# Graph attention on one core: maximum and exponentials of a unit one unit earlier, weighted sums in another PSUM bank, two bank pairs for the first group sums, slot rows zeroed during the projections

## What is computed

```python
h = layer_norm(node_feature, ln1_g, ln1_b)
qkv = (h @ Wqkv + bqkv).reshape(N, 3, H, DH)          # N 625, H 8, DH 64
q = qkv[:, 0] * D ** (-0.5); k = qkv[:, 1]; v = qkv[:, 2]
logits = jnp.einsum('ehd,ehd->eh', q[src], k[dst])    # per edge
a = logits + dist_attn + path_attn
mx = jax.ops.segment_max(a, dst, num_segments=N)
e = jnp.exp(a - mx[dst])
s = jax.ops.segment_sum(e, dst, num_segments=N)
msg = v[src] * (e / s[dst])[:, :, None]
agg = jax.ops.segment_sum(msg, dst, num_segments=N).reshape(N, D)
x = agg @ Wo + bo
```

## Time and profile before

| | us |
|---|---|
| median of 3 runs | 859.73 (856.99 to 859.93) |
| the profiled execution, its own time | 858.02 |
| its span, first to last instruction | 856.4 |
| projections, up to the barrier | 0 to 94.6 |
| attention, up to the next barrier | 94.6 to 357.7 |
| PE, DVE, ACT, POOL busy | 703.6, 524.8, 421.7, 162.2 |

### The profile page before, as it was taken

How to read it: one execution, slowest core, us unless ns; L and a number is a source line. 1 busy time by engine, 2 the same in 40 slices (tenths; PEclk the granted TensorE clock), 3 DMA queues, 4 the chain that set the end, 5 groups by cost and what they waited for, 6 DMA issues and landing times. The chain is left out here.

```text
span 856.4 us, 14647 instructions
## 1 busy us (share of the span) xinstructions
PE 703.6 (82%) x4980; PEld 550.1 (64%) x4980; DVE 524.8 (61%) x1107; ACT 421.7 (49%) x689; POOL 162.2 (19%) x242
## 2 busy tenths in 40 slices
PE   3997506676666767599999999999999999999993
PEld 2663203354444444348988867987889899988782
DVE  6658415587677733264432265527888788888864
ACT  5235202466666644256444364215676666766740
POOL 7342425455445310000000000310000000000022
PEclk9999765599999965699999999999999999999998
DMA  8232774555666454250000204395677666777224
GB/s 273 64 58 33 181 117 132 174 158 160 174 158 172 155 187 158 59 200 1 1 1 1 74 3 146 122 340 192 216 240 234 219 216 237 256 234 236 88 58 142
DMA packets 104125, 125.63 MB, mean 147 GB/s; under 512 B 32370, under 2 KB 70028, under 8 KB 103532
## 3 DMA queue, kind: packets, MB, share of 16 engines
q1 hardware_dynamic: 96955, 115.06, 42.8%
q0 software_dynamic: 5600, 6.54, 3.4%
q10 hardware_dynamic: 1488, 3.01, 1.5%
HBM read 94.91 MB, written 29.67 MB: 145 GB/s over the span
## 5 line engine op out<-in xcount | busy, mean ns | idle before, releaser
L2128 PE MATMUL ps<-xT,w_hi 128*128 128x480 f32 (+7 forms) x512 | 110.1, 337 | 2.4 <-DVE hT L1947 2.2
L1021 PE MATMUL ps<-onehot,group_weights 128*32 128x314 bf16 x1272 | 63.1, 341 | 43.8 <-ACT sums_out L976 23.9
L919 DVE TENSOR_SCALAR onehot<-iota_h,windows 128x628 bf16<-128x628 f16 x212 | 75.0, 417 | 32.1 <-DMA windows<-window_scratch 16.6
L2128 PEld LDWEIGHTS ps<-xT,w_hi 128*128 128x128 f32 x512 | 82.0, 189 | 9.9 <-DVE hT L1947 4.1
L1021 PEld LDWEIGHTS ps<-onehot,group_weights 128*32 128x32 bf16 x1272 | 36.8, 110 | 69.4 <-issue 42.2
L1933 DVE TENSOR_TENSOR w_lo<-weights_far,w_hi 128x1024 fp32r<-128x1024 f32 x64 | 78.0, 1220 | 2.5 <-ACT w_hi L2043 2.2
L2130 PE MATMUL ps<-xT,w_lo 128*128 128x240 f32 (+7 forms) x512 | 74.5, 268 | 0.0
L2130 PEld LDWEIGHTS ps<-xT,w_lo 128*128 128x128 f32 x512 | 73.5, 190 | 1.5
L976 ACT ACTIVATE sums_out<-ps 128x628 f32<-128x628 f32 x53 | 36.8, 695 | 70.8 <-PE ps L1021 50.4
L940 DVE CUSTOM_DVE_ANT_0 weights<-sums_in,exponents 126x628 f32<-126x628 f32 x40 | 34.4, 861 | 57.3 <-issue 30.8
L2043 ACT ACTIVATE w_hi<-weights_far 128x1024 fp32r<-128x1024 f32 x64 | 67.2, 1052 | 0.0
(11 more groups left out here) (308 smaller groups left out, 1551.7 us busy)
## 6 DMA issues: line engine op xcount, KB each, us to landing
weights_far<-in_L_ffn_w SPq DMA_DIRECT2D x64, 512.0 KB, 5.9
sums_scratch<-sums_out SPq DMA_DIRECT2D x53, 314.0 KB
weights_near<-in_L_ffn_w SPq DMA_DIRECT2D x32, 512.0 KB, 3.6
sums_in<-sums_scratch SPq DMA_DIRECT2D x40, 309.1 KB
weights_near<-in_L_gnn_W SPq DMA_DIRECT2D x4, 1024.0 KB, 5.5
weights_near<-in_L_ffn_sw SPq DMA_DIRECT2D x8, 512.0 KB, 5.2
weights_near<-in_L_gnn_Wqkv SPq DMA_DIRECT2D x3, 1024.0 KB, 7.6
weights_ff<-in_L_gnn_W SPq DMA_DIRECT2D x1, 3072.0 KB, 14.2
```

The costliest lines, as they stand in the source:

```text
L919: dve.tensor_scalar(onehot[w % 3][:, j, :], iota_h, windows[:, w % RING, j, 1:2], None, ALU.is_equal)\
L1021: last = pe.matmul(psW[r, a, :], R[w % 3][:, j, :, part], onehot[w % 3][:, j, a * SH:(a + 1) * SH], start=part == 0, stop=part == 2)
L2128: pe.matmul(both(bank, cap), w[u % 2][0][:, c, cut], xT(r)[:, c, :, :], start=c == 0, stop=False)
```

## The change

- The unit loop has another order. ACT does `norm(u)`, `exps(u+1)`, `keep(u)`, then the copies of the unit's blocks. DVE does `weights(u)`, for even u `collect(u//2 - 1)`, `guards(u+1)`, then the group weights of the next unit's blocks. PE does the sums of the first block, then logits for odd u or weighted sums for even u, then `turn(u)` (not `turn(u-1)`), then the sums of the second block.
- `psO` lies in bank 7, beside the end of `psP`. `turn` therefore waits for the collecting (`o_moved`), and `logits` no longer does; `weighted_sums` no longer waits for the next exponentials.
- The first 14 blocks of sums use two bank pairs in turn, 4 and 5, and 6 and 7. From block 14 on there is one pair as before. `turn(0)` waits for the 14 copies. `exps(0)` and `guards(0)` come behind block 1.
- In the projections the low parts of rounds 1 and 2 are made by DVE and not by POOL, and DVE, ACT and PE have small changes of order there (values of tile 2 earlier, exponentials of round 2 earlier, four filler matmuls in place of three). Only four blocks of windows are loaded there; blocks 4 and 5 follow in the attention.
- The slot rows are zeroed in three pieces that ACT issues between the copies of queries and keys.
- SP starts the attention with the two stores of edge parts. It waits for them only ahead of the first window that needs them (block 20), and the five parameter loads come behind all units.

```diff
+LOADED = 4
+ZERO_AT = {1: (0, 8), 5: (8, 16), 13: (16, SLOTS // DH)}
...
 @@ projections
-            for w in range(0, AHEAD, 2):
+            for w in range(0, LOADED, 2):
                 load_groups(nc, sp, mybir.EngineType.SP, w, tab, rec2_d, windows, g_in)
...
-            low_part(1)
-            low_part(2)
...
+            def low_part(r):
+                b0, nb = ROUNDS[r]
+                dve.wait_ge(mid_ready, r + 1)
+                dve.tensor_tensor(parts[:, b0:b0 + nb, :, 6:6 + 3 * H - 2:3], rec_all[:, b0:b0 + nb, :, 2:REC],
+                                  parts[:, b0:b0 + nb, :, 5:5 + 3 * H - 1:3], ALU.subtract).then_inc(lo_ready, 1)
...
             differences(2)
+            values(2)
+            rest_part(1)
             ends(2)
             longest_part()
-            values(2)
-            rest_part(1)
+            dve.wait_ge(lo_ready, 1)
+            low_part(1)
             values(3)
             rest_part(2)
             values(4)
+            low_part(2)
...
+                    if i in ZERO_AT:
+                        z0, z1 = ZERO_AT[i]
+                        act.dma_start(rows_d[z0 * DH:z1 * DH, :].rearrange("(a p) n -> p a n", p=DH),
+                                      zeros[0:DH, :].unsqueeze(1).broadcast_to([DH, z1 - z0, D])).then_inc(rows_zeroed, 16)
...
-            keep_awake(pe, psum[0], ident, iota_n, 3)
+            keep_awake(pe, psum[0], ident, iota_n, 4)
 @@ attention_units
-    psO = psum[0][:, 320:320 + TILE]
-    psW = banks[:, 4:6, 0:SH]
+    psO = psum[7][:, 256:256 + TILE]
...
+    leading = blocks_by(0)
+    def psW(w):
+        return banks[:, 6:8, 0:SH] if w < leading and w % 2 else banks[:, 4:6, 0:SH]
+    def stored_for(w):
+        return 16 * len(ROUNDS) if (w + 1) * GW > ROUND * GPB else 0
 @@ vector
-            for w in range(blocks_by(1)):
+            for w in range(2):
+                group_weights(w)
+            guards(0)
+            for w in range(2, blocks_by(1)):
                 group_weights(w)
             for u in range(UNITS_ALL):
-                ws = list(unit_blocks(u + 1))
-                guards(u)
-                for w in ws[0:1]:
-                    group_weights(w)
-                if u % 2 and u >= 3:
-                    collect((u - 3) // 2)
-                weights(u)
-                for w in ws[1:]:
-                    group_weights(w)
+                weights(u)
+                if u % 2 == 0 and u:
+                    collect(u // 2 - 1)
+                if u + 1 < UNITS_ALL:
+                    guards(u + 1)
+                for w in unit_blocks(u + 1):
+                    group_weights(w)
 @@ scalar
-        act.dma_start(rows_d[0:SLOTS, :].rearrange("(a p) n -> p a n", p=DH),
-                      zeros[0:DH, :].unsqueeze(1).broadcast_to([DH, SLOTS // DH, D])).then_inc(rows_zeroed, 16)
...
             for u in range(UNITS_ALL):
-                ws = list(unit_blocks(u))
-                for w in ws[0:1]:
-                    copied(w)
-                if u:
-                    keep(u - 1)
-                exps(u)
-                for w in ws[1:]:
-                    copied(w)
-                norm(u)
-            keep(UNITS_ALL - 1)
+                norm(u)
+                if u + 1 < UNITS_ALL:
+                    exps(u + 1)
+                keep(u)
+                for w in unit_blocks(u):
+                    copied(w)
 @@ tensor
-                wait_past(pe, w_copied, w)
+                wait_past(pe, w_copied, w - 1 if w < leading else w)
...
                 wait_past(pe, e_ready, 2 * q)
-                wait_past(pe, o_moved, q - 1)
...
                 wait_past(pe, pt_ready, u)
+                if u == 0:
+                    pe.wait_ge(w_copied, leading)
+                wait_past(pe, o_moved, u // 2)
...
                 pe.wait_ge(pt_ready, 2 * (q + 1))
-                pe.wait_ge(e_ready, min(2 * q + 3, UNITS_ALL))
...
             for u in range(UNITS_ALL):
                 ws = list(unit_blocks(u))
-                if u % 2 == 0 and u:
-                    logits(u // 2)
-                if u % 2 and u >= 3:
-                    weighted_sums((u - 3) // 2)
                 for w in ws[0:1]:
                     sums(w)
-                if u:
-                    turn(u - 1)
+                if u % 2 and u + 1 < UNITS_ALL:
+                    logits((u + 1) // 2)
+                if u % 2 == 0 and u:
+                    weighted_sums(u // 2 - 1)
+                turn(u)
                 for w in ws[1:]:
                     sums(w)
-            turn(UNITS_ALL - 1)
             weighted_sums(UNITS_ALL // 2 - 1)
```

More of the change, by code:

```diff
@@ L868, in unit_rows @@
                 sp.dma_start(sums_in[u % 3][0:TILE, :], rows[g0:g0 + TILE // GD, 0:GD, h, :]).then_inc(units_in[u % 3], 16)
-            blocks(range(blocks_by(0)))
+            for w in range(LOADED, AHEAD):
+                load(w)
+            blocks(range(window_blocks(0) + 1))
             unit_rows(0)
             unit_rows(1)
+            blocks(range(window_blocks(0) + 1, leading))
             for u in range(UNITS_ALL):
@@ L975, in copied @@
                 wait_past(act, out_done[w % 3], 16 * (w // 3))
[L976 removed]
+                act.activation(halves(sums_out[w % 3]), psW(w), ACT.Copy).then_inc(w_copied, 1)
             def exps(u):
@@ L1057, in _ @@
             logits(0)
-            for w in range(blocks_by(0)):
+            for w in range(leading):
                 sums(w)
```

73 lines of the change are left out of this document (39 added, 34 removed).

## The result

The changed kernel takes 918.97 us (median of 4 runs, 916.49 to 919.44) against 858.36 us (855.25 to 859.93) of the kernel before on the same chip: a ratio of 1.0705, 95% interval 1.0665 to 1.0745. It was forecast at 883 with a range of 856 to 902, so the sign was right and the size was not. The profiled execution took 916.49 us, 58.5 more than that of before (858.02).

The account below looks back on a forecast made before the run. The prediction took a chain through several engines to bound the kernel. From 858.02 us it added 27.4 for the attention up to the last unit, -1 and +0.5 behind it, and -2 in the next kernel: 883, range 856 to 902.

Parts of the forecast that it names:

- T0: First turning of a unit's weights, ending the leading blocks: forecast at 139 us (137 to 142), a gain of 24.5.
- the tail: Last nine units, without sums: forecast to take 34 us against 44.2, at mostly full clock.
- the end: Behind the last units, additions waiting for late parameter loads: 0.5 us (at most 4), less 1 for faster weighted sums.
- the 2 us of gain behind it: Kernel behind the attention: 2 us less, because it starts with PE closer to full clock.
- T30: Turning after thirty units with sums, the loop's end: forecast at 345 us, T0 at 139 plus 206.
- the ring: Unit loop: one chain through all engines, sums included; thirty units 182 us at full clock, 237 at half, 206 mixed.
- the 14.2 of pure half clock: Unit loop: a pair of units forecast to take 14.2 us at half clock, against 10.68 at full clock.
- the 7 us for group weights: Unit loop: added to 175 us for group weights slowed beside GpSimd products, giving 182 at full clock.
- rival 3: Unit loop: half clock for most of it (T30 at 375), or late group weights; 905 to 912 us, chance 0.10.
- rival 4: Leading blocks: edge-part stores alone hold back sums, losing up to 8 of 24.5; 892 us, chance 0.64 with the forecast.
- The projections' 3 us: Ahead of the attention: PE's end forecast at 88.4 us, 3 us gained, with the zeroing's cost about 0.
- Rival 2: Unit loop: maximum and exponentials run ahead, engines' own load sets the pace, thirty units 120; 796 us, chance 0.04.

Follow-up runs that it names:

- e6: The changed kernel with both the copy of a unit's first block ahead of the next exponentials and its group weights ahead of collecting and maximum: 824.46 us.
- e14: The changed kernel with a unit's first group weights moved ahead of collecting and maximum, plus four unread filler matmuls behind each of 30 turnings: 863.97 us.
- e4: The changed kernel with only the first block's group weights moved right behind the weights, ahead of collecting and the next maximum: 910.0 us.
- e9: The changed kernel with the old unit loop, and one bank pair instead of two in the leading blocks: 844.89 us, against 844.28 with two.
- e12: e6 with the slot rows zeroed in one transfer at the start of the attention: 834.71 us.
- e11: e6 with parameter loads after unit 24, results in bank 0, and the slot rows zeroed in six pieces at units 4 to 24: 824.53 us.
- e15: e6 with results kept in bank 7, parameter loads after unit 24, and the slot rows zeroed in six pieces at units 4 to 24: 821.65 us.
- e2: The changed kernel with only the copy of a unit's first block of sums moved ahead of the next exponentials and keep: 880.83 us.
- e3: The changed kernel with four unread filler matmuls of 192 columns behind each of the first 30 turnings: 869.32 us.
- e7: e6 with three unread filler matmuls of 192 columns behind each of the first 30 turnings: 827.84 us.
- e5: The changed kernel with all slot rows zeroed at step 13 of the projections and the parameter loads after unit 24: 917.1 us.

## Why the prediction was wrong, point by point

Forecast +24.9 us against the profiled execution, measured +58.5. Term by term: T0 came 2.4 later than 139, the loop took 27.1 more than 206, the tail 1.6 less than 34, the end 3.9 more (+3.4 for -0.5), and of the 2 us of gain behind it 1.7 were not there: 33.5 together. The prediction counted 39 blocks between T0 and T30; there are 38, and 36 in the kernel before.

1. **The failed step is the clock, "With half of the time at each level: 2 / (1/182 + 1/237) = 206".** The share was nearly right: 0.70 in the mean, which between 0.5 and 1.0 is 40% of the time at full clock, and the same mean with 40% would give 211. What failed is that the share was laid over the ring as a whole, as if the ring ran faster whenever the clock was full. The ring runs through PE's sums and the logits or weighted sums, and these were granted 0.50 and 0.65 or 0.63; the full clock fell to PE's gaps (0.92 and 0.95) and to the turnings (1.00), which lie beside the ring. So the loop took 233, close to the 237 of half clock. Against its steps at full clock, the pair above is longer by 0.77 us for each sums (178.80 - 177.11 for 0.92), 0.65 and 0.70 for the logits and weighted sums, and 0.47 for a late product (copy to next sums 1.31 for 0.84): 3.36 of the 3.35 measured. That it comes so near to the 14.2 of pure half clock is in part luck, since 14.2 has 1.0 twice for logits and weighted sums and nothing for the product. The 237 isn't built like the 182 either: it leaves out the 7 us for group weights and the 2 us off at the ends, with which it would be 242. The mechanism stood in rival 3, "T30 at 375 or so", whose 0.10 it shared with late group weights; T30 was at 374.55, and the kernel's time lies above that rival's 905 to 912 too.
2. **The order was right.** The sums in the ring, the copy behind keep, the single bank pair: e6 shows that moving two links out of it is worth 94 us with their clock. The sum of the links at full clock, 182, met the 181.5 measured with the clock held, but with luck: the fillers' own cost lies in the measured one, and the product was taken at 0.67 us and took 1.16, so that the group weights were given 2.96 us and needed 3.40 (173.71 to 177.11). The 7 us that the prediction added for them measured 3.4 at full clock (e14) and 9.5 without fillers (e4).
3. **The leading blocks were right**: the stall gone, pairs 4.9 to 5.3 us apart, the second bank pair worth nothing (e9). T0 at 141.43 is inside 137 to 142. The cause of the stall was told as the zeros alone; by e12 they bring back 8.44 of the 20.32 us, and SyncE's wait for the edge parts ahead of its first store of sums, which rival 4 named, was another part.
4. **The projections' 3 us were there but were paid away.** "Cost about 0" for the zeros was wrong: the first piece is issued at 34.23, ahead of the record loads (from 37.92), and DVE waits 14.46 us for them instead of 12.41. Take the zeros out, and the 3.0 us appear (e11, e12, e15).
5. **The end** cost 3.4 us more, inside the bound of 4. It was taken near 0 because only the additions were counted (to 408.20, before the weighted sums end at 411.43). What counts is the 8.2 us behind them. The weighted sums gained nothing: 2.37 us as before.
6. **The tail** was right: 32.4 for 34, at 0.92 of the clock.
7. **Rival 2** (796 us, the engines' own load) was refused because of the copy behind keep, rightly. It was to decide from where the copy no longer stands there; e2 moved the copy alone and took 880.8. The group weights had to leave too (e6), and then thirty units took 141.5 us, not 120.

The signs of being right nearly all appeared: no long gap, T0 near 139, the copy right behind keep, a clock that changes many times. None of them tells a ring at half clock from one at a mean clock; the spacing of the units does, 6.8 and 7.3 us here (173.94, 180.70, 187.97).

## What to carry to other kernels

Where a ring through several engines leaves TensorE gaps, work out its time at both clocks, and then ask which of TensorE's pieces lie in the ring and which clock they get: a mean over the stretch counts the clock that was granted while TensorE stood idle. Here the half-clock end was near (233 for 237), with the copy moved the loop came between the ends (e2, 0.81), and the loop of before kept the full clock with gaps of about 1.5 us, so neither end is a rule. When an operation is put one step ahead, look on each engine at what is queued behind it: here a copy and four one-hots of the next block stood behind a maximum and exponentials that wait for TensorE, and two small moves together turned +7% into -4%. Where two branches end within half a microsecond of each other, taking one away shows little; move both before judging either.

## What the runs showed of the hardware

- Added work made a kernel 50 us faster: four matmuls of 192 columns in each unit brought the clock from 0.70 to 0.99 and the loop from 233.1 to 181.5 us (e3). Once the ring was opened, three of them made the loop 6.3 us longer (e7).
- The granted clock and PE's work can stand against each other for 230 us: 0.70 in the mean, 0.92 in a gap of 2.4 us and 0.50 in the sums behind it, and a median sum matmul of 468 ns (293 at full clock).
- GpSimd's product takes 0.67 us alone (e4) and 1.16 when it starts 0.17 us behind DVE's weights.
- Transfers of zeros that nobody waits for still cost: with one of 1024 KB issued ahead of the record loads DVE waited 2.1 us longer for them, and with one of 2944 KB behind the first of them it stood idle for 6.22 us ahead of the second round (e5).
